# One decoder layer on one core: q and k turned together, rows and blocks placed by transfers, one factor on q, a third feed-forward bank, 2-byte turns

## What is computed

```python
x = _layernorm(x + attn(x))            # q,k,v = x @ w.T in 16 heads of 16; rope on q and k
#   scores = einsum('bshd,bstd->bsht', q, k) / 4 ; softmax over t ; attn = weights @ v ; @ wo.T
x = _layernorm(x + wkv(time_decay, time_first, k=x, v=ctx))     # recurrence over 128 tokens
x = _layernorm(x + ffn(x))             # quantised to 8 bits: silu(bitlinear(x, w1)) * bitlinear(x, w2), then w3
```

## Time and profile before

| | before |
|---|---|
| median of 3 runs | 302.68 us (302.1 to 304.95) |
| the profiled execution: its time | 304.7 us |
| its span, first to last instruction | 302.9 us |
| mean granted PE clock | 0.875 |
| busy share: PE, PEld, DVE, ACT, POOL | 73%, 49%, 81%, 53%, 56% |
| transfers | 12.33 MB, 11967 packets |

### The profile page before, as it was taken

The page is one execution under the profiler, slowest core; times in us unless marked ns, Lnnn a source line. Parts: engine busy times, 40 slices in busy tenths (PEclk is TensorE's granted clock), DMA queues, the critical chain, the costliest instruction groups (busy, mean ns, idle before and its releaser), DMA issues. The chain is left out here.

```text
span 302.9 us, 9905 instructions
## 1 busy us (share of the span) xinstructions
PE 219.7 (73%) x3778; PEld 149.3 (49%) x3778; DVE 245.3 (81%) x541; ACT 160.0 (53%) x345; POOL 169.9 (56%) x336
## 2 busy tenths in 40 slices
PE   3466969797978797979787978788888849462631
PEld 1344655575655565655555655555555536231310
DVE  2788688869989999999999999999999994846221
ACT  3125132628484848484848484848484846563421
POOL 2103167536767666766666666666667674754211
PEclk9759687759999999999999999999999987956555
DMA  7802010100202020202020202020201010000000
GB/s 225 299 0 56 1 56 0 54 2 4 69 3 71 2 71 4 73 2 71 2 73 3 71 2 74 2 71 2 71 4 53 5 52 3 17 1 19 0 17 17
DMA packets 11967, 12.33 MB, mean 41 GB/s; under 512 B 1872, under 2 KB 11152, under 8 KB 11920
## 3 DMA queue, kind: packets, MB, share of 16 engines
q1 hardware_dynamic: 11200, 11.67, 12.4%
q10 hardware_dynamic: 720, 0.03, 0.1%
HBM read 9.60 MB, written 2.10 MB: 39 GB/s over the span
## 5 line engine op out<-in xcount | busy, mean ns | idle before, releaser
L635 ACT ACTIVATE x<-res,nmr,rstd 128x256 f32<-128x256 f32 x32 | 19.2, 600 | 50.2 <-POOL nmr L743 50.2
L750 POOL TENSOR_TENSOR hid<-gate,up_s 128x352 f32<-128x352 f32 x32 | 29.8, 932 | 17.4 <-issue 9.4
L385 PE MATMUL ps_qk<-wqkv,xT 128*128 128x512 f32 x64 | 33.6, 652 | 4.8 <-DMA wqkv<-wqkv_in 4.8
L842 DVE STREAM_TRANSPOSE qkD<-qk_rot 128x1024 f32<-128x1024 f32 x16 | 30.8, 1927 | 7.3 <-POOL qk_rot L704 7.3
L738 POOL TENSOR_TENSOR var_eps<-mv,eps 128x1 f32<-128x1 f32 x48 | 11.5, 239 | 39.2 <-DVE mv L910 39.0
L726 POOL TENSOR_TENSOR frac<-state,now 128x512 f32<-128x512 f32 x16 | 19.0, 1187 | 25.6 <-DVE state L918 25.6
L417 PE MATMUL ps_s<-qkD 20*64 20x64 f32 x1024 | 25.8, 245 | 8.1 <-DVE qkD L842 4.8
L417 PEld LDWEIGHTS ps_s<-qkD 20*64 20x64 f32 x1024 | 21.5, 152 | 14.8 <-issue 8.4
L741 POOL TENSOR_TENSOR rstd<-var_eps,minus_half 128x1 f32<-128x1 f32 x48 | 26.4, 550 | 3.8
L614 ACT ACTIVATE th<-ps_a,half_gate 128x352 f32<-128x352 f32 x32 | 17.7, 553 | 20.3 <-PE ps_b L497 19.2
L924 DVE RECIPROCAL den_rec<-frac 128x256 f32<-128x256 f32 x16 | 27.9, 1745 | 0.0
(11 more groups left out here) (112 smaller groups left out, 622.6 us busy)
## 6 DMA issues: line engine op xcount, KB each, us to landing
xT<-xT_in SPq DMA_DIRECT2D x16, 128.0 KB, 2.3
ctxT<-ctxT_in SPq DMA_DIRECT2D x16, 128.0 KB, 2.2
x_res<-x_in SPq DMA_DIRECT2D x16, 128.0 KB, 2.4
out<-y_out SPq DMA_DIRECT2D x16, 128.0 KB, 1.7
w_raw<-w_in SPq DMA_DIRECT2D x2, 704.0 KB, 6.8
wqkv<-wqkv_in SPq DMA_DIRECT2D x2, 384.0 KB, 4.0
w_raw<-w_in SPq DMA_DIRECT2D x1, 640.0 KB, 8.5
wo<-wo_in SPq DMA_DIRECT2D x1, 256.0 KB, 5.0
```

The source lines that it names most:

```text
L385: last = mm(ps_qk[:], xT[k.slot][:, h, :], wqkv[:, h, 0:2 * C], start=h == 0, stop=h == 1)
L635: fn(dst[:], res[i][:], ACT.Identity, bias=nmr[i][:], scale=rstd[i][:]).then_inc(ln_done[i], 1)
L750: g.tensor_tensor(hid[:, half * FH:(half + 1) * FH], gate[half][:], up_s[half][:], ALU.mult).then_inc(hid_done, 1)
L842: v.transpose(qkD[k.slot][:].rearrange("p q (t h) -> p q h t", h=HEADS), qk_rot[:].rearrange("p (q h) d -> p q h d", q=2)).then_inc(qk_dma ...
```

## The change

- **q and k.** The rotation of q and k by the same angles leaves their product as it was but for cos^2 + sin^2. `rope` and `rotate` go; q alone is multiplied by a table turn_gain = cos^2 + sin^2 (`copy_q`, DVE, 256 columns), k and v are copied by one ACT copy of 512 columns (`copy_kv`). All three stand in qkv_tok: head by head 16 columns of q and 16 of k, and a row for v whose 16 columns ahead of the data hold a one and zeros.
- **The transpose.** One stream transpose of 512 columns (`turn_qk`) turns q and k together into qkT. `move_qk` on SP then copies q's rows and k's rows, 16 partitions by 2 KB each, into qkD: eight transfers per tile. The mask rows of qkD are loaded once (eight transfers issued by ACT at the start).
- **v.** `store_v` writes v's rows to a buffer in HBM (256 KB) and `spread_v` reads it back in eight transfers, each 16 partitions by 16 pieces of 128 bytes. `v_to_dmajor`, `block_v` and `copy_v_blocks` go.
- **2-byte turns.** POOL takes the rounding constant off (`whole_x`, 256 columns; `whole_h`, 704 columns) and writes bfloat16; `turn_xq` and `turn_hq` turn bfloat16, `copy_xq` and `copy_hq` are plain copies (one for hq).
- **Third bank.** `turn_hq` and `down` use a bank ps_c of their own.
- **Order.** DEPTH goes from 4 to 6 and all five lists are written in another order; work done once (sums, rounding) is tied to tile 0 by `once`.

```diff
-DEPTH = 4
+DEPTH = 6
...
+            def move_qk(k):
+                wait(sp, qk_turned, k.t + 1)
+                wait(sp, scores, k.t - 1)
+                for g in range(QUADS):
+                    for i in range(2):
+                        sp.dma_start(qkD[k.slot][PAD * g:PAD * g + HD, i, :],
+                                     qkT[PAD * g + HD * i:PAD * g + HD * (i + 1), :]).then_inc(qk_moved[k.slot], 16)
+            def store_v(k):
+                wait(sp, kv_copied, k.t + 1)
+                wait(sp, v_moved[k.slot], 16 * V_MOVES * k.pair)
+                sp.dma_start(v_rows[k.slot], qkv_tok[:, 1]).then_inc(v_stored[k.slot], 16)
+            def spread_v(k):
+                wait(sp, v_stored[k.slot], 16 * (k.pair + 1))
+                wait(sp, heads_out, k.t - 1)
+                src = v_rows[k.slot].rearrange("(b x l) h d -> x l h b d", x=4, l=2)
+                for x in range(4):
+                    for l in range(2):
+                        sp.dma_start(v_blk[k.slot][2 * HEADS * x + l:2 * HEADS * (x + 1):2], src[x, l]
+                                     ).then_inc(v_moved[k.slot], 16)
...
+                on(at(-1), load_xT)
+                on(at(2), load_x)
+                on(at(1), spread_v)
+                once(at(0), load_ffn_weights)
+                on(at(0), store_v)
+                on(at(2), load_ctx)
+                on(at(6), store)
+                on(at(0), move_qk)
...
             def score(k):
-                wait(pe, qk_dmajor, k.t + 1)
+                if k.t == 0:
+                    constants()
+                wait(pe, qk_moved[k.slot], 16 * MOVES * (k.pair + 1))
...
+            def copy_kv(k):
+                wait(act, kv_projected, k.t + 1)
+                wait(act, qk_turned, k.t)
+                wait(act, v_stored[1 - k.slot], 16 * ((k.t + 1) // 2))
+                fn(qkv_tok[:, :, :, HD:2 * HD].rearrange("p i h d -> p (i h) d"),
+                   ps_kv.rearrange("p (g d) -> p g d", d=HD), ACT.Copy).then_inc(kv_copied, 1)
...
+            def whole_h(k):
+                wait(pool, h_scaled, k.t + 1)
+                wait(pool, hq_turned, k.t)
+                g.tensor_scalar(hq16[:, 0:HIDDEN], hq32[:], -MAGIC, 1.0, ALU.add, ALU.mult).then_inc(h_whole, 1)
...
+            def copy_q(k):
+                wait(dve, q_projected, k.t + 1)
+                wait(dve, qk_turned, k.t)
+                v.tensor_tensor(qkv_tok[:, 0, :, 0:HD].rearrange("p h (a i) -> p h a i", i=HH),
+                                ps_q.rearrange("p (h a i) -> p h a i", a=2, i=HH),
+                                turn_gain[:].unsqueeze(1).unsqueeze(1).broadcast_to([P, HEADS, 2, HH]),
+                                ALU.mult).then_inc(q_copied, 1)
+            def turn_qk(k):
+                wait(dve, q_copied, k.t + 1)
+                wait(dve, kv_copied, k.t + 1)
+                wait(dve, qk_moved[1 - k.slot], 16 * MOVES * ((k.t + 1) // 2))
+                v.transpose(qkT[:].rearrange("p (y h l) -> p h y l", h=HEADS, l=2), qkv_tok[:, 0]
+                            ).then_inc(qk_turned, 1)
```

More of the change, by code:

```diff
@@ L84, in on, with once @@
         stage(tile, *which)
-class Due:
-    def __init__(self):
-        self.begun = set()
-    def __call__(self, what, tile):
-        if tile is None or what in self.begun:
-            return False
-        self.begun.add(what)
-        return True
+def once(tile, stage, *which):
+    if tile is not None and tile.t == 0:
+        stage(*which)
 def decoder_layer(nc, x_in, xT_in, ctxT_in, wqkv_in, wo_in, w1_in, w2_in, w3_in,
-                  freq_in, decay_in, first_in, ident_in, pads_in, pos_in, out):
+                  freq_in, decay_in, first_in, ident_in, mask_in, pos_in, out):
     with ExitStack() as ctx:
@@ L944, in gate_up @@
             def gate_up(k, half):
[L946 to L947 removed]
+                wait(dve, tanh_done[half], k.t + 1)
+                wait(dve, hid_done[half], k.t)
                 v.scalar_tensor_tensor(gate[half][:], th[half][:], 1.0, ps_a[:, 0:FH], ALU.add, ALU.mult
[L949 removed]
+                                       ).then_inc(gate_done[half], 1)
             def amax_of_h(k):
[L952 removed]
+                for half in range(2):
+                    wait(dve, hid_done[half], k.t + 1)
                 wait(dve, c_h_done, k.t)
@@ new lines, in step @@
+                on(at(6), scale_of_h)
+                on(at(2), max_quads)
+                on(at(2), max_rows)
+                on(at(2), max_hi_part)
+                once(at(3), cut_weights, 2)
+                on(at(2), max_lo_part)
+                on(at(4), recip_den)
+                on(at(5), gate_up, 0)
+                on(at(3), residual, 0)
+                on(at(6), scale_of_out)
+                on(at(3), moments, 0)
+                once(at(2), weight_scales)
+                on(at(3), mean_var, 0)
@@ new lines, in step @@
+                on(at(1), turn_qk)
+                on(at(4), residual, 1)
+                on(at(5), gate_up, 1)
+                on(at(4), moments, 1)
+                on(at(6), residual, 2)
+                on(at(4), mean_var, 1)
+                on(at(6), moments, 2)
+                on(at(5), amax_of_h)
+                once(at(2), cut_weights, 0)
+                on(at(2), heads_to_tokens)
+                once(at(0), wkv_tables)
+                on(at(5), floor_h)
+                on(at(2), recip_sums)
@@ L1052, in _ @@
+                on(at(4), amax_of_x)
+                on(at(0), copy_q)
+                on(at(4), floor_x)
+                on(at(2), normalise)
+                on(at(4), recip_x)
+                once(at(2), cut_weights, 1)
+                on(at(3), scan)
+                on(at(6), mean_var, 2)
+                once(at(1), weight_sums)
+                on(at(5), recip_h)
             run_steps(step)
```

407 lines of the change are left out of this document (169 added, 238 removed).

## The result

The changed kernel is slower by 13%. Over executions taken in turn on one chip, before took 302.43 us in the median (302.1 to 304.95, 4 runs) and the changed kernel 342.61 us (341.32 to 346.34, 4 runs), a ratio of 1.131 with a 95% interval of 1.125 to 1.137. The prediction said 275 us, 262 to 297, and gave "slower" 15 in 100. The chip has a faster and a slower state, and medians of several executions are of the faster one alone, which leaves out two of four executions of the kernel e9_early_residual, near 270 us.

A forecast was written before the change was run, and what follows sets the result against it. DVE's sum was taken to bound the kernel before, and a loop through moves, PE, ACT and DVE after. The span, 15.5 + 15 x 13.4 + 58 = 274.5 us, gave a forecast of 275 us, range 262 to 297.

The forecast's parts named there:

- DVE's sum: DVE's work per full step: said to bound the kernel before, falling from 15.03 to 12.17 us.
- The ring: Loop once per step from transpose through moves, scores, project_kv, up, tanh and gate_up to the next transpose: 13.4 us.
- The moves: SP's eight move_qk transfers, from the transpose's end to the last landing: 5.1 us, bounds 4.5 and 6.9.
- The landing: Time from a move_qk transfer's issue on SP until its data has arrived: 2.0 us, bounds 1.7 and 2.3.
- The spacing: Distance between successive move_qk issues on SP: 0.44 us, bounds 0.40 and 0.66.
- with all bounds high: Full step if moves take 6.9 us and the transpose 1.05: 15.4 us.
- drain: Stretch behind the last transpose of q and k: 58 us instead of 64.0, bounds 55 and 66.
- an idle stretch ahead of the scores of about a microsecond: Sign expected on PE in the changed kernel's profile, ended by a transfer of qkD.
- SP's list as the bound: Rival: SP's 21 issues per step become the bound; at 0.75 us each, 312 us; chance 0.08.
- The packets: Rival: small packets fill the 16 transfer engines; 17.5 us per step, 339 us in all; chance 0.07.
- The moves are slower, not ruinous: Rival: issue spacing 0.5 to 0.6 or landings of 2.5 us and more; about 290 us; chance 0.22.
- The small terms: Minor prices: transpose 0.90 us, turn_xq 0.20, POOL's whole_x 0.27 and whole_h 0.74; weigh_v never waiting for v_blk.

The follow-up runs named there:

- e9_early_residual: Changed kernel without moves (two transposes write qkD), and for the last tile layer norm 0's three DVE operations ahead of the first gate_up; 262.0 us.
- e7: e6 plus 12 idle bf16 matmuls of 128 columns on PE ahead of its wait for the moves; 259.4 us.
- e1_warm: Changed kernel plus 12 idle float32 matmuls on PE ahead of its wait for the moved q and k; 313.6 us.
- e6: Changed kernel with the same q and k bytes moved in two strided transfers of 64 rows instead of eight of 16; 262.8 us.
- e4: Changed kernel with spread_v's eight transfers of 128-byte pieces left out from tile 2 on; 347.3 us.
- e10: Changed kernel with the eight move_qk transfers reading the same-sized rows from a DRAM tensor instead of qkT; 319.1 us, one run.
- e3: Changed kernel with every stage from the scores on, plus spread_v and the loads, one step later (DEPTH 7); 318.7 us.

## Why the prediction was wrong, point by point

- **What bounded the kernel before**, DVE's sum, was read rightly: e7 brought the steady step to 12.15 us, with 12.17 predicted for DVE's work after the change. The agreement is a little better than the terms, since the transpose took 0.71 and not 0.90.
- **The ring** was right in its order and its members, and the end of the first transpose came as predicted (15.4 us, predicted 15.5). The structure was not the mistake; two terms were.
- **The moves, "0.03 + 7 x 0.44 + 2.0 = 5.1 us"**, measured 7.13, beyond even the upper bound of 6.9. The landing was right (1.95). The spacing was (157.92 - 152.81) / 7 = 0.73 us: 0.63 as the normal distance and 0.7 us for one long issue. The step that failed is the choice of row: 0.44 came from a transfer of another kind, DRAM to SBUF, while the sentence treated an issue as one thing. I kept 0.66 as the upper bound, though the same group had a row of 0.97, put aside as crowded. At 0.73 the prediction's own formula gives a step of 15.4, which is slower than the 15.03 of before; 15.5 + 15 x 15.4 + 58 is 304.5 us, so this term alone takes the whole forecast gain of 28 us away. (The same 15.4 stood in the prediction as the step "with all bounds high"; the range, which ended at 297 us, left it out.) e1_warm measured a mean step of 15.39 and a drain of 64.5, and is 3% slower than before: with most of the clock given back the sign is that of the moves and of the drain.
- **PE's durations** were all read at the granted clock of 1.00 of the earlier trace rows, and carried over to a kernel in which PE waits for transfers once per step. This was no term of the sum, no bound and no rival. It cost 2.75 us in the step shown, and at least 2.19 in the mean and 29 us in all by e1_warm, where the clock still fell in three steps. The Trainium skill (TensorE: Matmul & The Clock Gate, "HAM oscillation — how this bites in real kernels") describes a loop that waits for a transfer in each turn and starts every turn at the low clock; the trace agrees, by 0.92 in the wait and 0.50 behind it. The prediction even asked for "an idle stretch ahead of the scores of about a microsecond"; by e6 even such a wait is a risk.
- **The two terms feed each other**: a longer batch makes PE wait longer, and that makes the members behind the wait dearer. Hence the range was not a matter of a wider bound on one price.
- **The rivals.** SP's list as the bound was not what happened, but its condition (0.67 us between issues on the ring) was met. The packets fell with e4. "The moves are slower, not ruinous" had the right term and stopped at 0.6; its reason, other transfers that share the queue, is not what e4 and e10 show.
- **The small terms** held: transpose 0.71 (0.67 to 1.05 given), `turn_xq` 0.11 (0.14 to 0.27 given), POOL's new operations 0.60 and 0.78 (0.27 and 0.74: the first is off by twice, hidden), `weigh_v` never waiting for v_blk.
- **The drain**, 65.5 for 58. The heads of the last tile came 19.3 us behind its transpose, 15.5 was predicted; 1.9 of the miss are the moves (from the transpose to the scores 6.95 us for 5.1) and 0.9 the scores at the low clock. Behind the heads nothing was gained. DVE of the changed kernel, last tile (heads, scan, residual 1, first `gate_up`, residual 2):

```profile
298.37 0.70 DVE L890 STREAM_TRANSPOSE o_tok<-ps_o 128x512 f32<-128x512 f32 x1
...
312.10 1.29 DVE L935 TENSOR_TENSOR_SCAN state<-w_tab,past 128x516 f32<-128x516 f32 x1
...
319.82 0.42 DVE L911 TENSOR_TENSOR res<-ps_w,x 128x256 f32<-128x256 f32 x1 [2.06 <-PE ps_w L408]
...
328.49 0.52 DVE L965 SCALAR_TENSOR_TENSOR gate<-th,ps_a 128x352 f32<-128x352 f32 x1 [3.65 <-ACT th L637]
...
339.36 0.48 DVE L915 SCALAR_TENSOR_TENSOR res<-ps_c,s_out,x 128x256 f32<-128x256 f32 x1 [5.10 <-PE ps_c L546]
```

  and the same of before, whose heads stand in the earlier trace rows at 256.85:

```profile
267.62 1.74 DVE L918 TENSOR_TENSOR_SCAN state<-w_tab,past 128x516 f32<-128x516 f32 x1 [0.97 <-POOL past L711]
...
276.30 0.42 DVE L896 TENSOR_TENSOR res<-ps_w,x 128x256 f32<-128x256 f32 x1 [1.33 <-PE ps_w L377]
```

  Scan to residual 1 fell from 8.7 to 7.7 us (2.2 promised for `recip_den`), and the feed-forward part by 1.9 us (3 less 1.8 promised). But heads to scan grew from 10.8 to 13.7 us. The new lists put waits for older tiles' feed-forward between the heads and the scan (`gate_up` on DVE at 305.75, and by e9 `hidden` on POOL); since taking one of them out of DVE's list gained nothing, how the 2.9 us divide is not shown. I had only listed the waits that the change takes away there, not those that it adds.

## What to carry to other kernels

A transfer put between two engines on a loop costs its landing and one issue for every piece, at the price of its own kind of source and target; count the pieces first, and fold them into one strided transfer if the layout allows it (342.6 us with eight, 262.8 with two). Then ask what the waiting engine does meanwhile: a matmul duration read at full clock holds only if PE stays busy, and where PE will wait for data once per turn, price all its members behind the wait at the lower clock as well, or give it idle matmuls. And before a list is blamed or a wait taken away, follow the next list: the waits of e3 and e9 were only moved.
